# A fused attention and expert kernel on one core: prologue work redistributed, and the spread of the low inverses issued by GpSimd

## The reference

```python
x = x + jnp.tanh(g_xattn[0]) * _L0_xattn_ref(_layernorm(x, axis=-1), ctx_2048, ctx_2048)
x = x + jnp.tanh(g_ffn[0]) * _L0_ffn_ref(_layernorm(x, axis=-1), L0_ffn_wg, L0_ffn_W, L0_ffn_b)
# _L0_xattn_ref: 16-row heads, qk = einsum('bdm,bdn->bmn') * scale, softmax over n, einsum('bmn,bcn->bcm')
# _L0_ffn_ref: logits = xt @ wg; idx = argmax; gate = probs[idx]; out = gate * (W[idx] @ xt + b[idx])
```

## Time and profile before

| | us |
|---|---|
| median of 3 runs | 541.4 (539.82 to 543.08) |
| profiled execution | 542.39 |
| its span in the trace | 540.5 |
| TensorE busy | 496.1 (92%) |
| VectorE busy | 433.2 (80%) |
| ScalarE busy | 348.8 (65%) |
| GpSimd busy | 346.0 (64%) |

### The profile page before, as it was taken

How to read it: one execution, slowest core, us unless ns; L and a number is a source line. 1 busy time by engine, 2 the same in 40 slices (tenths; PEclk the granted TensorE clock), 3 DMA queues, 4 the chain that set the end, 5 groups by cost and what they waited for, 6 DMA issues and landing times.

```text
span 540.5 us, 10090 instructions
## 1 busy us (share of the span) xinstructions
PE 496.1 (92%) x2580; PEld 176.9 (33%) x2580; DVE 433.2 (80%) x851; ACT 348.8 (65%) x428; POOL 346.0 (64%) x531
## 2 busy tenths in 40 slices
PE   0289999999999999999998999999999999899993
PEld 0012223332333333333323232333333245444451
DVE  5799889888898989899998899898989868334341
ACT  3216878878788888888886879887777942111110
POOL 7536466677676767767667778886448556645541
PEclk9999999999999999999999999999999999999998
DMA  4887366576665756676657667675546555644310
GB/s 130 224 193 230 104 178 185 142 234 179 180 208 177 215 168 202 198 230 168 198 153 217 198 178 209 178 194 173 148 122 209 151 175 190 191 149 136 103 61 0
DMA packets 51761, 92.96 MB, mean 172 GB/s; under 512 B 22899, under 2 KB 24947, under 8 KB 51689
## 3 DMA queue, kind: packets, MB, share of 16 engines
q1 hardware_dynamic: 36624, 67.33, 44.2%
q0 software_dynamic: 10560, 24.93, 14.2%
q10 hardware_dynamic: 4536, 0.23, 0.6%
HBM read 68.96 MB, written 28.41 MB: 180 GB/s over the span
## 4 chain that ended last, share of the span: by engine, by line
PE 44%; DVE 13%; DMA 13%; SPq 12%; issue 7%; POOL 5%; ACT 3%; ACTq 1%; DVEq 0%; POOLq 0%
PE ps_pv L1394 11%; PE ps_scores L1455 10%; PE ps_ring L1352 10%; PE ps_scores L1371 9%; SPq L369 5%; DMA recip_dram<-sums 4%; DVE neg_max L1206 3%; DVE neg_max L958 3%; SPq L406 3%; SPq L362 2%; DMA sums<-high_num 2%; DMA parts_dram<-prep 2%; DMA scale<-recip_dram 1%; ACT probs L859 1%; DMA stacks<-shift_parts 1%
## 5 line engine op out<-in xcount | busy, mean ns | idle before, releaser
L958 DVE TENSOR_REDUCE neg_max<-ps_ring 128x1 f32<-128x512 f32 x480 | 307.0, 682 | 25.8 <-PE ps_ring L1352 24.7
L859 ACT ACTIVATE probs<-ps_scores 128x1024 f32<-128x1024 f32 x256 | 251.3, 1022 | 57.3 <-PE ps_scores L1371 52.9
L1352 PE MATMUL ps_ring<-stacks 96*128 96x512 bf16 x480 | 165.6, 383 | 3.5 <-DVE neg_max L958 2.4
L1371 PE MATMUL ps_scores<-stacks 128*128 128x512 bf16 x512 | 153.0, 381 | 2.1 <-ACT probs L859 0.8
L1394 PE MATMUL ps_pv<-probs,v_ones 128*32 128x512 f32 x992 | 132.1, 605 | 0.0
L1352 PEld LDWEIGHTS ps_ring<-stacks 96*128 96x128 bf16 x480 | 46.3, 96 | 153.3 <-DVE neg_max L958 106.1
L1455 PE MATMUL ps_scores<-w_sb,f_xt 128*128 x184 | 83.4, 595 | 1.6 <-ACT f_xt L835 1.4
L1371 PEld LDWEIGHTS ps_scores<-stacks 128*128 128x128 bf16 x512 | 48.1, 100 | 53.4 <-ACT probs L859 13.2
L835 ACT COPY f_xt<-ps_scores 128x512 f32<-128x512 f32 x22 | 12.9, 584 | 67.6 <-PE ps_scores L1438 59.9
L1455 PEld LDWEIGHTS ps_scores<-w_sb,f_xt 128*128 128x128 f32 x184 | 32.9, 190 | 34.1 <-issue 34.1
L566 POOL TENSOR_TENSOR prep<-prep 128x512 f32<-128x512 f32 x30 | 34.7, 1159 | 10.6 <-ACT prep L806 10.6
(11 more groups left out here) (144 smaller groups left out, 492.1 us busy)
## 6 DMA issues: line engine op xcount, KB each, us to landing
stacks<-parts_dram SPq DMA_DIRECT2D x224, 64.0 KB, 3.0
parts_dram<-prep POOLq DMA_DIRECT2D x15, 768.0 KB
w_sb<-w_t SPq DMA_DIRECT2D x16, 512.0 KB, 3.4
recs_dram<-rec SPq DMA_DIRECT2D x16, 512.0 KB
stacks<-parts_dram SPq DMA_DIRECT2D x32, 192.0 KB, 3.2
prep<-x_perm SPq DMA_DIRECT2D x16, 256.0 KB, 2.7
prep<-k_perm SPq DMA_DIRECT2D x16, 256.0 KB, 2.9
v_in<-v_t SPq DMA_DIRECT2D x16, 256.0 KB, 3.0
```

The costliest lines, as they stand in the source:

```text
L859: nc.scalar.activation(probs[:, k % 2, 2 * jp:2 * jp + 2], ps_scores[:, jp], ACT.Exp).then_inc(exp_done, 1)
L958: nc.vector.tensor_reduce(neg_max[:, g, j, c:c + 1], ps_ring[:, SLOT[tile]], AX.X, ALU.max, negate=True).then_inc(ring_free, 1)
L1352: nc.tensor.matmul(ps_ring[:, SLOT[tile]], q_stack[0:KS, into.p, g, j, c * 128:(c + 1) * 128], k_stack[0:KS, into.p, g, j], start=True, st ...
L1371: last = nc.tensor.matmul(ps_scores[:, jp, j % 2], k_stack[0:KA, B.p, g, j, c * 128:(c + 1) * 128], q_stack[0:KA, B.p, g, j], start=True, ...
```

## The change

Four things are different. In the main loop the four transfers that spread the low inverses are issued by GpSimd (`spread_low`), ahead of `add_low` in the next batch; SP keeps the high ones (`spread_high`) and stores the low inverses ahead of the rows and keys of B+4. In the prologue three of the six query transfers of the first stack are issued by ScalarE, the second stack of batch 1 is loaded behind the first shift, and VectorE's two memsets of `recs` stand between its split instructions. For the last batch VectorE adds the high half straight from PSUM (`add_last_high`); ScalarE's copy of it is gone. In the tail GpSimd's scatters of slots 1 and 2 go behind the third table read, and the second table's columns are taken two slots later.

```diff
-            def load_query_stack(B, g):
+            def load_query_stack(B, g, terms=range(TERMS)):
 
                 mine = parts_dram[bass.ds(B.b, 1)].rearrange("o s t (c g j) m -> s (o g) t c (j m)", g=NG, j=NJ)
-                for term, t in enumerate(QUERY_PARTS):
-                    sp.dma_start(q_stack[term * DH:(term + 1) * DH, B.p, g].rearrange("p j m -> p (j m)"), mine[0, g, t]
-                                 ).then_inc(stack_in[B.p][g], 16)
+                for term in terms:
+                    sp.dma_start(q_stack[term * DH:(term + 1) * DH, B.p, g].rearrange("p j m -> p (j m)"),
+                                 mine[0, g, QUERY_PARTS[term]]).then_inc(stack_in[B.p][g], 16)
...
-                wait(sp, (low_added, x1_done)[g], B.b)
+            def spread_high(B):
+
+                wait(sp, x1_done, B.b)
                 if not isinstance(B.b, int):
                     stand_alone(sp)
-                sp.wait_ge(recips_out[g], B.b * 16 + 16)
+                sp.wait_ge(recips_out[1], B.b * 16 + 16)
                 stand_alone(sp)
                 for j in range(NJ):
-                    at = 32 * j + g * DH
-                    sp.dma_start(scale[at:at + DH, g], recip_dram[g, j].partition_broadcast(DH)).then_inc(recips_in[g], 16)
+                    at = 32 * j + DH
+                    sp.dma_start(scale[at:at + DH, 1], recip_dram[1, j].partition_broadcast(DH)).then_inc(recips_in[1], 16)
...
             load_key_stack(Batch(0, 0), 0)
             sp.wait_ge(queries_out, 16)
-            load_query_stack(Batch(0, 0), 0)
+            load_query_stack(Batch(0, 0), 0, range(TERMS // 2))
             load_key_stack(Batch(0, 0), 1)
             load_query_stack(Batch(0, 0), 1)
             load_rows_keys(Batch(1, 0))
...
             sp.dma_start(stacks[KS:KA, 1].rearrange("p s g j m -> p (s g j m)"),
                          stacks[KS:KA, 0].rearrange("p s g j m -> p (s g j m)")).then_inc(pads_in, 16)
-            for g in range(NG):
-                load_stack(Batch(0, 1), g)
+            load_stack(Batch(0, 1), 0)
             load_values(Batch(0, 1))
             sp.wait_ge(pads_in, 16)
             load_shift(Batch(0, 0), 0)
+            load_stack(Batch(0, 1), 1)
             load_rows_keys(Batch(1, 1))
...
                 if prev and by_transfer(B.plus(-1)):
                     store_recips(B.plus(-1), 1)
                     load_weight(B)
-                    spread_recips(B.plus(-1), 1)
+                    spread_high(B.plus(-1))
...
@@ -481,11 +481,10 @@
                     load_stack(B.plus(2), 0)
                 if not B.known(NB - 1):
                     load_shift(B.plus(1), 0)
+                if by_transfer(B):
+                    store_recips(B, 0)
                 if not isinstance(B.b, int) or B.b + 4 < NB:
                     load_rows_keys(B.plus(4))
-                if by_transfer(B):
-                    store_recips(B, 0)
-                    spread_recips(B, 0)
...
+            def spread_low(B):
+
+                wait(pool, low_added, B.b)
+                if not isinstance(B.b, int):
+                    stand_alone(pool)
+                pool.wait_ge(recips_out[0], B.b * 16 + 16)
+                stand_alone(pool)
+                for j in range(NJ):
+                    pool.dma_start(scale[32 * j:32 * j + DH, 0], recip_dram[0, j].partition_broadcast(DH)).then_inc(recips_in[0], 16)
...
                 if prep:
                     rstd1(B.plus(3))
                 if prev:
+                    spread_low(B.plus(-1))
                     add_low(B.plus(-1))
...
             for s in range(NSLOT):
-                first = s + NREC == FIRST_LATE
                 if s == 2:
                     number_places(3)
                     store_tokens(*GROUPS[3])
-                if first:
-                    scatter(s)
                 if s + NREC == PHASES[1][1]:
                     pool.wait_ge(cols_ready, 2)
                     records_stored(GROUPS[2][1])
                 if s + NREC == FIRST_LATE:
+                    scatter(s)
                     pool.wait_ge(cols_ready, 3)
                     records_stored(NB)
                 if s + NREC < NSLOT:
                     gather(s + NREC)
-                if not first:
-                    scatter(s)
                 if s == 2:
                     read_slots(2)
+                    scatter(s - 1)
+                if s != 1 and s + NREC != FIRST_LATE:
+                    scatter(s)
...
-                if B.known(NB - 1):
-                    act.wait_ge(high_turned, NB - TURNED)
                 wait(act, x1_done, B.b)
-                nc.scalar.mul(high_num[:], last_bank if B.known(NB - 1) else ps_pv[:], (high_gate if by_transfer(B) else high_only)[:]).then_inc(high_read, 1)
+                nc.scalar.mul(high_num[:], ps_pv[:], (high_gate if by_transfer(B) else high_only)[:]).then_inc(high_read, 1)
...
+            def load_first_queries(g, terms):
+
+                act.wait_ge(queries_out, 16)
+                mine = parts_dram[0:1].rearrange("o s t (c g j) m -> s (o g) t c (j m)", g=NG, j=NJ)
+                for term in terms:
+                    act.dma_start(q_stack[term * DH:(term + 1) * DH, 0, g].rearrange("p j m -> p (j m)"),
+                                  mine[0, g, QUERY_PARTS[term]]).then_inc(stack_in[0][g], 16)
...
             for n in range(1, 3):
                 B = Batch(n // 2, n % 2)
                 cast_high(B, 1)
+                if n == 1:
+                    load_first_queries(0, range(TERMS // 2, TERMS))
                 norm1(B)
...
             for s in range(NSLOT):
-                if s == 1:
-                    read_high(Batch(7, 1))
                 if s == 2:
                     norm2(Batch(7, 1))
...
+            rec_steps = [lambda: nc.vector.memset(recs[:, 0:2].rearrange("p r n -> p (r n)"), 0.0),
+                         lambda: nc.vector.memset(recs[:, 2:4].rearrange("p r n -> p (r n)"), 0.0)]
             steps = [lambda: nc.vector.memset(low_half[:], 0.0)]
             steps += [lambda j=j: nc.vector.memset(low_half[32 * j:32 * j + DH], 1.0) for j in range(NJ)]
             steps += [lambda: nc.vector.tensor_scalar(high_half[:], low_half[:], -1.0, 1.0, ALU.mult, ALU.add),
-                      lambda: nc.vector.memset(recs[:, 0:2].rearrange("p r n -> p (r n)"), 0.0),
-                      lambda: nc.vector.memset(recs[:, 2:4].rearrange("p r n -> p (r n)"), 0.0),
                       lambda: nc.vector.memset(up_to[:], 0.0),
                       lambda: nc.vector.memset(taken[:], 0.0)]
...
             first_low(1)
+            set_constants(rec_steps[:1], STACK_CONSTS)
             first_rest(0, qn)
             first_low(0)
+            set_constants(rec_steps[1:], STACK_CONSTS + 1)
             stats1(Batch(0, 1))
             mean1(Batch(0, 1))
             dve.wait_ge(gates_ready, 1)
-            set_constants(steps, STACK_CONSTS)
+            set_constants(steps, STACK_CONSTS + 2)
...
+            def add_last_high():
+
+                dve.wait_ge(low_read, NB)
+                chain.add(nc.vector.scalar_tensor_tensor(num[:], last_bank, high_only[:], low_num[:], ALU.mult, ALU.add))
+
             def add_attention(B):
 
-                dve.wait_ge(high_read, B.b + 1)
-                chain.add(nc.vector.tensor_tensor(num[:], low_num[:], high_num[:], ALU.add))
+                if not B.known(NB - 1):
+                    dve.wait_ge(high_read, B.b + 1)
+                    chain.add(nc.vector.tensor_tensor(num[:], low_num[:], high_num[:], ALU.add))
...
             last = Batch(7, 1)
             turn_sums(last, 1)
             invert_sums(last, 1)
+            add_last_high()
             take_logits(last.plus(-1))
             turn_back(last)
             add_attention(last)
...
                 if s == 2:
                     take_logits(last)
                     find_experts(3)
+                    take_columns(1)
                     find_gates(3)
                     take_ranks(3, ps_ring[:, 0, RANK_AT:])
...
                 if s == 0:
                     name_experts(1)
                     take_tiles(1)
-                    take_columns(1)
```

3 lines of the change are left out of this document (1 added, 2 removed).

## The result

The changed kernel takes 591.9 us (median of 7 runs, 586.4 to 605.2), the kernel before 541.9 beside it (7 runs, 539.8 to 546.9): ratio 1.088, 95% interval 1.084 to 1.093. I had forecast 558 and a range up to 575. The direction was right, the size was not: +50 us, where the forecast had +16.6. Five of the seven runs took 586.4 to 595.1 us (mean granted clock 0.959 to 0.977); the other two, 603.4 us (0.955) and 605.2 us (0.944), are slow ones that the ratio leaves out, and the trace shown here is of the last, so its batches are longer than those of the median run.

A forecast was written before the change was run, and what follows sets the result against it. TensorE was taken to set the loop's pace, so only lateness reaching it costs time. Loop +20.0, prologue -2.4 and tail -1.0 gave +16.6 us: 558 us for the median, range 546 to 575.

The forecast's parts named there:

- margin of 2.07 us: Main loop, batch 7: how late the low product may start before VectorE waits at its statistics line for GpSimd's last sum.
- factor 0.9: Main loop: about 0.9 of VectorE's wait at the statistics line becomes idle time of TensorE.
- D: Main loop: how much later GpSimd's low product starts because of the four moved transfers; forecast 4.0 us, from 3.3 to 5.5.
- my loop term: Main loop: loss from the late low product, 22.0 us over the batches less 2.0 us TensorE already idled, 20.0 us.
- the rule: Main loop: each batch costs 0.9 x (D - margin), with a margin of 2.07 us in batch 7.
- my term: Main loop, batches 9 to 14: forecast loss of 8.4 us from the late low product.
- The high scale's wait: Main loop, GpSimd at L598: the 0.89 us wait for the high inverses would go, since they now arrive first.
- the limit that I had called the weaker one: Main loop: the shift for TensorE's next batch comes late once D is beyond 2.9 us.
- upper bound of 5.5: Main loop: largest D in us, with SP's slowest landing of 3.4 us and 0.6 us waiting ahead of the first issue.
- rival (2): Main loop: GpSimd's transfer lands in 5.17 us every time, D is 6.9, the time 589 us; chance 0.04.
- The term of -2.4 us: Prologue: VectorE's memsets moved and query issues shared with ScalarE bring the first maximum and batch 0's first scores 2.4 us sooner.
- The -1.0 us of the tail: Tail: scatters behind the third table read let the gather start sooner, cutting TensorE's idle; gain 1.0 us (0 to 1.8).

The follow-up runs named there:

- delay kernel with a D of 3.6 to 3.9: The kernel before plus a GpSimd memset of all of recs ahead of each low product, no transfer moved: 563.8 us, ratio 1.040.
- kernel with the longest delay: The kernel before plus GpSimd memsets of one and a half times recs ahead of each low product, no transfer moved: 594.2 us, ratio 1.098.
- kernel that clears all of recs: The same run as the delay kernel with a D of 3.6 to 3.9, against the kernel before: 563.8 us, ratio 1.040.
- kernel with the shortest delay: The kernel before plus a GpSimd memset of half of recs ahead of each low product, no transfer moved: 551.6 us, ratio 1.017.

## Why the prediction was wrong

**The mechanism was right as far as it went.** The lateness of the low product reaches TensorE through VectorE's statistics, with the margin of 2.07 us and the factor 0.9. The delay kernel with a D of 3.6 to 3.9 takes 563.8 us, against the 561 to 562 of my loop term alone. That it comes so near is in part luck: batches 1 to 8 cost 2 us less than the rule, the later ones 4.5 us more than my term. The high scale's wait went, as said, and in the changed kernel's trace TensorE never waits for the shift, the limit that I had called the weaker one.

**The step that failed is the size of D.** I took "1.5 + 1.9 + 0.2 (nops and wait) + 0.4, for the weight load", 4.0 us, with an upper bound of 5.5. It measured 4.9 to 6.5 in batches 1 to 8. The issues were right, and the wait ahead of the first was 0.2 to 0.6 us. The mis-sized term is the landing, 1.9 + 0.4 = 2.3 us: it measured 3.1 to 4.5 us in batches 1 to 8, and 1.9 to 2.1 us once the weight load, and with it SP's high spread, was out of its way. So the 0.4 should have been 1.2 to 2.6 us. My upper bound used SP's slowest landing, 3.4 us. That was a landing in a place where SP had ordered its transfers by itself. The 5.17 us landing of GpSimd's own, in the same rows, was the nearer row: same queue, beside a large load. I gave it to rival (2) at 0.04 with "in the loop only the weight load runs beside". That load, with the high spread behind it, was enough for landings of up to 4.5 us. Rival (2), 589 us, is within 3 us of what came, but by luck: it had a D of 6.9, where the mean was 5.8, and no fall of the clock, which made up the difference.

The rule of the Trainium skill (DMA: Bandwidth & Descriptors, Specifications), about 0.4 us more to the first byte for a DMA issued by GpSimd, is neither borne out nor refuted: with the weight load moved GpSimd's spreads landed after 1.9/2.1/2.6 us (min/median/max), where SP's before took 1.7/1.9/3.4. The medians are 0.2 us apart, and the traffic beside them was not the same.

**A term was missing.** I had TensorE's lost time as idle time alone. Behind idle stretches of mostly 2.65 us its granted clock fell to the 1.2 GHz level for some microseconds, at 1.3 to 2.9 us a batch in the kernel with the longest delay. Of the 42.2 us of batches 1 to 8 the rule with the measured D gives 26.6. The rest, 15.6, is the growth of TensorE's busy time: 212.3 us in these eight windows, against 196.5 in the same batches of the kernel that clears all of recs, at full clock. This is the longest of the seven executions, with the lowest clock. In the profiled runs of the kernel with only the transfers moved and of the longest delay, the rest is 8.6 and 9.8 us, and TensorE's busy time has grown by 9.4 and 11.5; a median run of the changed kernel should be nearer to these. At a D of 3.6 to 3.9 batches 1 to 8 kept their clock, so a forecast at D = 4.0 rightly had none of it there, though batches 9, 11 and 13 fell; the error of D brought it into the others. That ScalarE's read of the low half waits as well (1.25 us of TensorE's idle) was also unseen, but in batch 2 the two together come to what the rule says: 1.25 + 2.66 = 3.9, against 0.9 x (6.5 - 2.07) = 4.0.

**The later batches.** In the profiled runs batches 9 to 13 cost 0.9, 3.0, 7.0, 6.2 and 3.3 us more than before; I had 0.9, 0.2, 3.3, 4.0 and 0. D is 4.2 to 5.5 there up to batch 12, batches 11 and 12 ran at 0.89, 10 and 13 at 0.94, and as the kernel with the shortest delay shows, these batches charge even a D of 1.9, where I had given two of them margins of 3 us and more.

**The ends.** The term of -2.4 us had the first pair at 20.0; it came at 21.54. The stack's issues now end at 17.84, 0.6 us sooner than before as I had it, but TensorE starts 3.7 us after them, not 2.1. The first of the six issues is 0.7 us later than before (16.49 against 15.81), and the transfers land after 2.6 to 4.0 us each, where SP's six took 2.2 to 2.4: issuing them in 1.4 us instead of 2.6 didn't make them land faster one behind the other. The gain of 1.1 us at the first scores, and 1.95 us at the first turn with the prologue alone, then went into the wait for k_perm. I had written that batch 1's parts would be put off by about 1 us and that this stays hidden; SP's loads of them came 3.8 us later (31.20 against 27.36), and it did not. The -1.0 us of the tail can't be told from nothing (541.0 against 542.1, ratio 1.001).

## What to carry to other kernels

A small transfer on the path of a waiting engine is priced by what runs beside it at that moment, so take the slowest landing of a like transfer beside a like load as the estimate, not as a far bound. Test a suspected lateness with a plain delay before arguing about the transfer: memsets of three sizes ahead of the low product gave the price curve. And price idle time of TensorE in two steps, first the wait, then the granted clock behind it.

## What the runs showed of the hardware

- TensorE's granted clock behind one idle stretch of 2.33 to 2.66 us in a batch: five of eight batches fell to 0.94 or 0.89, three stayed at 1.00. Stretches of 0.89 to 1.58 us left it at 1.00 in batches 1 to 8 of another kernel, whose batch 13 fell to 0.94 with none above 0.98 us.
- The last of four 32 KB broadcasts issued by GpSimd landed in 1.9 to 2.1 us (eight batches) with SP's 512 KB weight load moved away, and in 3.1 to 4.5 us beside it, 4.29 us with the load issued 0.7 us ahead; SP's own spread of the same size was also near.
- Four such transfers cost GpSimd 1.9 to 2.0 us of issuing per batch. The transfers at the end of each batch cost 9.5 us of kernel time; a plain delay of that length there cost 2.3 us, which the intervals don't tell from nothing.
